# An attention phase whose chances are divided by their sum before they are split and transposed, not after

## The chip, the core and the metric

The kernel runs on one core of a Trainium2 chip. The metric is the device time of one execution in microseconds (us); the kernel before takes 1757.22 us in the median of three runs (1755.55 to 1758.23). A measurement of this kernel can tell about 0.2%, 3.5 us, from no change.

The names of the engines are those of the profile: PE is TensorE's matmul and PEld its weight load, DVE is VectorE, ACT is ScalarE, POOL is GpSimd and SP is SyncE, which here only issues DMAs ("SPq"). Each engine takes its instructions strictly in the order of the program; an instruction that waits for a semaphore holds all behind it on its engine.

## The reference

Four sequences ("batches") of 512 tokens of width 1024, with 64 context tokens each, pass through cross attention and a quantised gated network, each behind a layer norm and with a residual:

```
x = x + attention(layernorm(x), context)      # 16 heads of 96, 4 groups of keys and values
x = x + ffn(layernorm(x))                     # weights and activations rounded to 8-bit steps, inner width 2752

hidden = concatenate([context, latents])      # 64 + 512 rows
q = latents @ Wq.T ; k = hidden @ Wk.T ; v = hidden @ Wv.T
attn = softmax((q . k) / sqrt(96))            # 512 x 576 for each head
out  = (attn . v) @ Wo.T

s = max(max(|t|) / 127, 1e-8)                 # fake_quant, row by row
q = clip(round(t / s), -128, 127) * s
```

## The kernel before, in words

The program has two phases with a barrier between them: `attention_phase` (until 1248 us of the profiled execution) and `ffn_phase`. The change lies in the first.

**Precision.** Matrix operands are float16 pairs: a value is written as a high part and the rest, a low part, and a product of two such operands is three matmuls (hi.hi, hi.lo, lo.hi). So everything that TensorE reads has to be split: ScalarE writes the high half (an `activation` with a float16 output), VectorE or GpSimd subtracts it from the float32 value and writes the low half.

**Work of a batch.** `batch_order(b)` writes TensorE's order out by hand, in 18 steps. Step j holds the four score tiles of head j (`score_tile`, 128 queries against 576 keys, into two PSUM tensors `ps_s` in turn), the product of the chances of head j - 2 with the values (`pv_tile`, into the one bank `ps_o`), and side work that fills the time: projections of values, queries and keys for later heads or for the next batch and the output projection of finished groups (`V`, `Q`, `K`, `WO`), in three banks `ps_g`. The first score tile stands first in a step, the others at quarters of the step's remaining work. Steps 16 and 17 have no scores.

**A tile of chances** passes: scores in `ps_s` -> VectorE's row maximum (L1113) -> ScalarE's exp in float32 into `p_f`, of which there are NF = 2, with the row's sum (L1006) -> ScalarE's exp a second time, in float16, into `p_nat` (L1012), after which the score bank is free -> GpSimd's subtraction in two pieces (L791, L792) -> a DMA transpose of the pair, from SP, into `pT` (L686). `p_nat` has NN = 4 places, so a tile's place is that of the same tile of the head before, and L1012 waits until that one's transpose has landed. The chances aren't yet divided by their sum. That is done at the end of a head: the reciprocals of the four sums (L1120) go to DRAM (`inv_out`, L690) and come back spread over 96 partitions (`inv_in`, L697, which waits on SP for the write's landing), and VectorE multiplies the head's output by them (`normalise`, L1131); then the output is split by ScalarE (L1021) and GpSimd (`out_lo`, L797).

**Weights of the second phase** are quantised beside this, in 52 units (`("w", g)`): SP loads a unit into one of two buffers `w_in` (`stage`), VectorE finds its scale (L1143 to L1154), ScalarE divides and adds a constant that rounds (`lift`, L976), VectorE takes the constant off and writes `w_int` (`round`, L1161), SP transposes it (`turn`, L641) and writes the result to DRAM (`keep`, L652). There is one `w_int`, so L1161 waits until the transpose before has landed. The weights of the attention pass the same two buffers in batch 0 (`split`, `cache`).

**The order on each engine** is a sorted list: `engine_events()` gives each operation a planned time, worked out from a rough cost of TensorE's own work (`pe_times`), and each engine executes its operations in the order of their planned times. `stage_events()` plans the weights, `token_events()` the layer norm, split and transpose of the next batch's tokens, which fall around step 11. These times only set the order; what an operation waits for are its semaphores.

**TensorE's waits** at the places touched: a score tile waits for `p_done` of the tile two before it (L902), the first `pv_tile` of a head for its four transposes and for `ps_o` to be free (L917 to L919).

## Time and profile before

| | |
|---|---|
| median of three runs | 1757.22 us (1755.55 to 1758.23) |
| the profiled execution | 1757.65 us |
| its span, first to last instruction | 1755.9 us |
| attention phase, to the border | about 1248.7 us |
| PE busy | 1567.4 us (89% of the span) |
| DVE, ACT, POOL busy | 1036.7, 655.3, 515.5 us |
| mean granted clock of TensorE | 0.955 |

How to read it: "busy" is the time in which an engine had an instruction in work. The clock is given as a share of 2.4 GHz and has two levels, 1.00 and 0.50 (1.2 GHz); a figure between them is a mean over a stretch. A "DMA share" is the mean busy share of the core's 16 DMA engines; it can pass 1 a little, since packets overlap. A wait is told as "who waited <- for what", with the sum, the number of times and the longest. SP issues DMAs, so the time of an "SPq" row is that of the issue, not of the transfer.

### The profile page before, as it was taken

The numbers are of one execution on the slowest core, as the hardware profiler recorded it, in microseconds if no ns is written. First come the engines' busy times: TensorE is split into PE (matmuls) and PEld (weight loads), VectorE is DVE, ScalarE is ACT, GpSimd is POOL, SyncE is SP. The second block draws the span as 40 slices with busy tenths as digits, with TensorE's granted clock in tenths as the row PEclk, the third lists the DMA queues.
The fourth block names the chain that finished last, engine by engine and source line by source line (L and its number), as shares of the span: only waits on it lengthen the run. The fifth ranks groups of instructions, "written<-read, shape, count | busy, mean of one in ns | idle before, by whom it ended". The sixth has DMA issues, their size and how long they took to land. (4 is left out here: it accounts for less than half of the span.)

```text
span 1755.9 us, 23588 instructions
## 1 busy us (share of the span) xinstructions
PE 1567.4 (89%) x8084; PEld 773.3 (44%) x8084; DVE 1036.7 (59%) x1760; ACT 655.3 (37%) x1180; POOL 515.5 (29%) x635
## 2 busy tenths in 40 slices
PE   6989989999877999888799788898579999999997
PEld 3544434654333465443346334443234444444443
DVE  5346554345555434555444445465379999898984
ACT  3456553256544225555422455452211111111110
POOL 3356653045445214445521244452000000000000
PEclk9999999999898999999999899999789999999998
DMA  7499999699999969999986999998863333324232
GB/s 233 116 249 237 240 231 233 185 212 228 226 227 230 200 173 222 239 209 230 222 200 187 263 218 205 207 202 199 263 227 85 91 89 86 95 80 105 70 93 64
DMA packets 546185, 323.62 MB, mean 184 GB/s; under 512 B 484144, under 2 KB 491056, under 8 KB 544944
## 3 DMA queue, kind: packets, MB, share of 16 engines
q1 hardware_dynamic: 546096, 322.49, 77.2%
q8 instruction: 50, 0.82, 0.2%
q14 instruction: 39, 0.32, 0.1%
HBM read 151.78 MB, written 46.79 MB: 113 GB/s over the span
## 5 line engine op out<-in xcount | busy, mean ns | idle before, releaser
L791 POOL TENSOR_TENSOR p_nat<-p_f,p_nat 128x512 f16<-128x512 f32 x256 | 300.6, 1174 | 478.9 <-ACT p_nat L1012 478.4
L1113 DVE TENSOR_REDUCE small<-ps_s 128x1 f32<-128x576 f32 x256 | 192.8, 754 | 257.2 <-PE ps_s L908 255.7
L907 PE MATMUL ps_s<-k,q 96*128 96x512 f16 x768 | 231.2, 393 | 95.4 <-ACT p_nat L1012 95.4
L1006 ACT ACTIVATE p_f<-ps_s,small 128x576 f32<-128x576 f32 x256 | 189.2, 739 | 267.5 <-DVE small L1113 265.5
L1012 ACT ACTIVATE p_nat<-ps_s,small 128x576 f16<-128x576 f32 x256 | 188.5, 736 | 133.3 <-DMA pT<-p_nat 132.7
L1391 PE MATMUL ps_gu<-w_gu_sb,xT 128*128 128x512 bf16 (+1 forms) x1152 | 230.8, 361 | 0.0
L1432 ACT ACTIVATE g_sb<-g_sb,sx 128x512 f32<-128x512 f32 (+1 forms) x128 | 74.5, 582 | 390.6 <-DVE g_sb L1503 331.5
L1404 PE MATMUL ps_d<-w_dn_sb,hT 128*128 128x512 bf16 x704 | 161.5, 383 | 5.4 <-DMA hT<-h_int 5.4
L907 PEld LDWEIGHTS ps_s<-k,q 96*128 96x128 f16 x768 | 76.2, 99 | 201.7 <-issue 82.1
L1391 PEld LDWEIGHTS ps_gu<-w_gu_sb,xT 128*128 128x128 bf16 x1152 | 112.8, 98 | 115.4
L922 PE MATMUL ps_o<-pT,v_lo 128*96 128x512 f16 x320 | 133.4, 417 | 33.0 <-DMA pT<-p_nat 32.9
L908 PE MATMUL ps_s<-k,q 96*128 96x64 f16 x768 | 150.1, 196 | 0.0
L818 PE MATMUL ps_g<-wo,o 128*128 128x512 f16 x384 | 148.9, 388 | 1.1 <-POOL o L797 1.1
L819 PE MATMUL ps_g<-wo,o 128*128 128x512 f16 x384 | 148.6, 387 | 0.0
L820 PE MATMUL ps_g<-wo,o 128*128 128x512 f16 x384 | 148.5, 387 | 0.0
L818 PE MATMUL ps_g<-xnT,wq 128*128 128x512 f16 x384 | 146.3, 381 | 1.4 <-DMA xnT<-xh 0.7
L820 PE MATMUL ps_g<-xnT,wq 128*128 128x512 f16 x384 | 146.2, 381 | 0.0
L819 PE MATMUL ps_g<-xnT,wq 128*128 128x512 f16 x384 | 146.1, 380 | 0.0
L1370 POOL TENSOR_TENSOR rstd<-var_eps,minus_half 128x1 f32<-128x1 f32 x16 | 8.8, 550 | 460.1 <-DVE var_eps L1473 460.1
L1174 DVE SCALAR_TENSOR_TENSOR x_acc<-ps_g,x_acc 128x512 f32<-128x512 f32 x128 | 88.1, 689 | 86.7 <-PE ps_g L820 86.5
L797 POOL TENSOR_TENSOR o<-o_tmp,o 96x512 f16<-96x512 f32 x64 | 75.6, 1182 | 194.8 <-ACT o L1021 194.8
L923 PE MATMUL ps_o<-pT,v_hi 128*96 128x512 f16 x320 | 130.1, 407 | 0.0
(113 smaller groups left out, 2403.6 us busy)
## 6 DMA issues: line engine op xcount, KB each, us to landing
w_in<-w_gu SPq DMA_DIRECT2D x40, 512.0 KB, 4.7
wq<-wq_c SPq DMA_DIRECT2D x36, 512.0 KB, 4.9
wo<-wo_c SPq DMA_DIRECT2D x24, 768.0 KB, 5.6
inv_sum<-inv_d SPq DMA_DIRECT2D x64, 192.0 KB, 3.4
gu_q<-w_t SPq DMA_DIRECT2D x44, 256.0 KB, 4.1
w_in<-w_dn SPq DMA_DIRECT2D x8, 1376.0 KB, 7.1
w_gu_sb<-gu_q SPq DMA_DIRECT2D x3, 2816.0 KB, 12.8
x_acc<-x SPq DMA_DIRECT2D x4, 2048.0 KB, 8.9
```

The source lines that it names most:

```text
L791: nc.gpsimd.tensor_tensor(n[:, S + C:2 * S], f[:, 0:T], n[:, 0:T], ALU.subtract)
L818: nc.tensor.matmul(o, l_hi, r_hi, start=(first and i == 0), stop=False)
L819: nc.tensor.matmul(o, l_hi, r_lo, start=False, stop=False)
L820: mm = nc.tensor.matmul(o, l_lo, r_hi, start=False, stop=(last and i == len(pairs) - 1))
L907: nc.tensor.matmul(o[:, 0:T], l, k2[0:HD, hl, kv, 0:T], start=(i == 0), stop=(i == 2))
L908: mm = nc.tensor.matmul(o[:, T:S], l, k2[0:HD, hl, kv, T:S], start=(i == 0), stop=(i == 2))
L922: nc.tensor.matmul(o, v_lo[:, t, kv, :], p[:, t, :], start=(t == 0), stop=False)
L1006: nc.scalar.activation(p_f[:, t % NF, :], scores(t), ACT.Exp, bias=bias, accum_out=sums[:, j % 2, t:t + 1])
L1012: nc.scalar.activation(p_nat[:, t % NN, 0:S], scores(t), ACT.Exp, bias=bias).then_inc(p_done, 1)
L1113: nc.vector.tensor_reduce(neg_max[:, j % 2, t:t + 1], scores(t), AX.X, ALU.max, negate=True).then_inc(mx_done, 1)
L1391: mm = nc.tensor.matmul(ps_gu[n % NR][:, 0:nu * P], xT[:, k, :], w[:, u0:u0 + nu, k, :], start=(k == 0), stop=(k == KD - 1))
L1404: mm = nc.tensor.matmul(ps_d[h][:], hT[0:rows, c, :], w_dn[0:rows, 4 * h:4 * h + 4, c, :], start=(c == 0), stop=(c == IC - 1))
```

## The change

- **Chances.** The exp is done once, in float32, into one of four `p_f` (NF = 4), and frees the score bank. VectorE scales the row's sum by 2^-9 and takes its reciprocal (`invert`, now for each tile). ScalarE multiplies `p_f` by it and writes the float16 high half (`high`); GpSimd multiplies `p_f` by it in place, in float32, and then subtracts the high half. What is transposed is divided already, times 2^9.
- **Output.** `normalise`, `inv_out`, `inv_in`, `o_tmp`, the broadcast sums and the DRAM tensor are gone. ScalarE writes the high half of a head's output straight from `ps_o`, VectorE (not GpSimd) the low half.
- **Semaphores.** The splits of attention weights have their own pair (`h_up`, `h_out`) and no longer share a count with the units' `w_up` and `w_out`. `pv_tile` waits for `o_lo_s`, not for `o_mul`.
- **Order.** Planned times are later for the units' `round`, `turn` and `keep` (six microseconds, `LAND`, for each landing), for tokens (an interval of 10 in place of 8, a start 8 earlier) and for the load of output weights; the units of the last batch are planned within 0.85 of its time.

```diff
-NF = 2
+NF = 4
...
+P_UP = 2.0 ** 9
+WEIGHTS_FOR = (1.0, 1.0, 1.0, 0.85)
...
-            units.append((START[b] + (i + 0.4) * (START[b + 1] - START[b]) / UNITS[b], ("w", g)))
+            units.append((START[b] + (i + 0.4) * WEIGHTS_FOR[b] * (START[b + 1] - START[b]) / UNITS[b], ("w", g)))
...
+LAND = 6.0
+TOKEN_LEAD, TOKEN_STEP = 20.0, 10.0
...
+        for h in range(halves):
+            k = TURNS.index((g, h))
+            t = max(t, turned[-1] + LAND)
+            dve.append((t, "round", g, h))
+            wide = halves == 2 or (k and halves_of(TURNS[k - 1][0] % NUNIT) == 2)
+            t = max(t + 2.5, (kept[-1] if wide else kept[-2]) + LAND)
+            sp += [(t, "turn", k), (t + LAND, "keep", k)]
+            turned.append(t)
+            kept.append(t + LAND)
...
-                act.append((t + 1.0, "exp", b, j, k))
-                pool.append((t + 3.0, "low", b, j, k))
-                sp.append((t + 5.0, "turn_p", b, j, k))
-                if k == TT - 1:
-                    dve.append((t + 3.3, "invert", b, j))
-                    sp += [(t + 3.8, "inv_out", b, j), (t + 6.5, "inv_in", b, j)]
+                dve.append((t + 2.0, "invert", b, j, k))
+                act += [(t + 1.0, "exp", b, j, k), (t + 2.4, "high", b, j, k)]
+                pool.append((t + 3.1, "low", b, j, k))
+                sp.append((t + 6.0, "turn_p", b, j, k))
...
-                dve.append((t + 0.1, "normalise", b, j))
-                act.append((t + 1.4, "out_hi", b, j))
-                pool.append((t + 2.2, "out_lo", b, j))
+                act.append((t + 0.1, "out_hi", b, j))
+                dve.append((t + 0.9, "out_lo", b, j))
...
             def chances_lo(b, j, t):
-                f, n = p_f[:, t % NF, :], p_nat[:, t % NN, :]
-                pool.wait_ge(p_done, tile(b, j, t) + 1)
-                nc.gpsimd.tensor_tensor(n[:, S + C:2 * S], f[:, 0:T], n[:, 0:T], ALU.subtract)
-                nc.gpsimd.tensor_tensor(n[:, S:S + C], f[:, T:S], n[:, T:S], ALU.subtract).then_inc(p_low, 1)
...
+                f, h = p_f[:, t % NF, :], p_nat[:, t % NN, :]
+                pool.wait_ge(p_high, tile(b, j, t) + 1)
+                nc.gpsimd.tensor_tensor(f, f, inv_sum[:, j % 2, t:t + 1].broadcast_to([P, S]), ALU.mult).then_inc(p_scaled, 1)
+                pool.wait_ge(p_scaled, tile(b, j, t) + 1)
+                nc.gpsimd.tensor_tensor(h[:, S + C:2 * S], f[:, 0:T], h[:, 0:T], ALU.subtract)
+                nc.gpsimd.tensor_tensor(h[:, S:S + C], f[:, T:S], h[:, T:S], ALU.subtract).then_inc(p_low, 1)
...
-                nc.scalar.activation(p_f[:, t % NF, :], scores(t), ACT.Exp, bias=bias, accum_out=sums[:, j % 2, t:t + 1])
+                nc.scalar.activation(p_f[:, t % NF, :], scores(t), ACT.Exp, bias=neg_max[:, j % 2, t:t + 1],
+                                     accum_out=sums[:, j % 2, t:t + 1]).then_inc(p_done, 1)
+
+            def chances_hi(b, j, t):
+
+                act.wait_ge(inv_done, tile(b, j, t) + 1)
                 if head(b, j):
                     act.wait_ge(p_turned[t], head(b, j) * EV)
...
-                nc.scalar.activation(p_nat[:, t % NN, 0:S], scores(t), ACT.Exp, bias=bias).then_inc(p_done, 1)
+                nc.scalar.activation(p_nat[:, t % NN, 0:S], p_f[:, t % NF, :], ACT.Copy,
+                                     scale=inv_sum[:, j % 2, t:t + 1]).then_inc(p_high, 1)
...
+            def invert(b, j, t):
+                dve.wait_ge(p_done, tile(b, j, t) + 1)
+                s = sums[:, j % 2, t:t + 1]
+                nc.vector.tensor_scalar(s, s, 1.0 / P_UP, None, ALU.mult).then_inc(sum_down, 1)
+                dve.wait_ge(sum_down, tile(b, j, t) + 1)
+                nc.vector.reciprocal(inv_sum[:, j % 2, t:t + 1], s).then_inc(inv_done, 1)
+
+            def out_lo(b, j):
+                hi, lo = out_rows(j)
+                dve.wait_ge(o_hi_s, head(b, j) + 1)
+                nc.vector.scalar_tensor_tensor(lo, ps_o[0:HD, :], 1.0 / P_UP, hi, ALU.mult, ALU.subtract).then_inc(
+                    o_lo_s, 1)
```

**VectorE, last batch, between two row maxima of head 2** (`small<-ps_s` is the row maximum, `small<-w_in` and `s_w<-small` the scale of a unit, `w_int<-w_in` the rounding, `q<-ps_g` and `o_tmp<-ps_o` evacuations). Before:

```order
L1113 TENSOR_REDUCE small<-ps_s 128x1
L1103 SCALAR_TENSOR_TENSOR q<-ps_g,q 128x512
L1143 TENSOR_REDUCE small<-w_in 128x1
L1161 TENSOR_SCALAR w_int<-w_in 128x1344
L1113 TENSOR_REDUCE small<-ps_s 128x1
L1131 TENSOR_TENSOR o_tmp<-ps_o,inv_sum 96x512
L1143 TENSOR_REDUCE small<-w_in 128x1
L1149 TENSOR_TENSOR small<-small 128x1
L1152 TENSOR_SCALAR s_w<-small 128x1
L1154 RECIPROCAL small<-s_w 128x1
```

In the changed kernel, from the same maximum on (L1112 is the maximum, L1118 and L1120 the new reciprocal, L1156 the rounding, L1125 the output's low half):

```order
L1112 TENSOR_REDUCE small<-ps_s 128x1
L1102 SCALAR_TENSOR_TENSOR q<-ps_g,q 128x512
L1138 TENSOR_REDUCE small<-w_in 128x1
L1144 TENSOR_TENSOR small<-small 128x1
L1147 TENSOR_SCALAR s_w<-small 128x1
L1149 RECIPROCAL small<-s_w 128x1
L1118 TENSOR_SCALAR small<-small 128x1
L1120 RECIPROCAL small<-small 128x1
L1156 TENSOR_SCALAR w_int<-w_in 128x1344
L1112 TENSOR_REDUCE small<-ps_s 128x1
L1125 SCALAR_TENSOR_TENSOR o<-ps_o,o 96x512
L1118 TENSOR_SCALAR small<-small 128x1
```

The rounding moved behind the scale's small steps and a reciprocal that waits for the exp; it still stands in front of the same maximum.

**SP, the same stretch** (`pT<-p_nat` are the transposes of chances, `w_t<-w_int` those of weights). Before:

```order
L641 DMA_TRANSPOSE w_t<-w_int 128x11x128
L622 DMA wq<-wq_c 128x2048
L690 DMA inv_d<-small 128x4
L686 DMA_TRANSPOSE pT<-p_nat 128x9x128
L652 DMA dn_q<-w_t 128x1408
L697 DMA inv_sum<-inv_d 96x512
L641 DMA_TRANSPOSE w_t<-w_int 128x11x128
L600 DMA w_in<-w_gu 128x1024
L686 DMA_TRANSPOSE pT<-p_nat 128x9x128 x2
```

In the changed kernel:

```order
L651 DMA_TRANSPOSE w_t<-w_int 128x11x128
L689 DMA x_acc<-x 128x4x1024
L696 DMA_TRANSPOSE pT<-p_nat 128x9x128
L632 DMA wq<-wq_c 128x2048
L662 DMA dn_q<-w_t 128x1408
L696 DMA_TRANSPOSE pT<-p_nat 128x9x128 x2
L651 DMA_TRANSPOSE w_t<-w_int 128x11x128
L610 DMA w_in<-w_gu 128x1024
```

The write and the read of the reciprocals are gone from the queue; the transposes of weights stand further apart from each other.

**SP, the last rows of the attention phase** (`dn_q<-w_t` is `keep`, `x<-x_acc` the store of the result). Before:

```order
L641 DMA_TRANSPOSE w_t<-w_int 128x11x128
L652 DMA dn_q<-w_t 128x1408
L722 DMA x<-x_acc 128x4x512
L641 DMA_TRANSPOSE w_t<-w_int 128x11x128
L652 DMA dn_q<-w_t 128x1408
L722 DMA x<-x_acc 128x4x512
L641 DMA_TRANSPOSE w_t<-w_int 128x11x128
L652 DMA dn_q<-w_t 128x1408
L641 DMA_TRANSPOSE w_t<-w_int 128x11x128
L652 DMA dn_q<-w_t 128x1408
```

In the changed kernel:

```order
L662 DMA dn_q<-w_t 128x1408
L639 DMA wo<-wo_c 128x3072
L651 DMA_TRANSPOSE w_t<-w_int 128x11x128
L639 DMA wo<-wo_c 128x3072
L662 DMA dn_q<-w_t 128x1408
L651 DMA_TRANSPOSE w_t<-w_int 128x11x128
L720 DMA x<-x_acc 128x4x512
L662 DMA dn_q<-w_t 128x1408
L720 DMA x<-x_acc 128x4x512
```

Two transposes and two writes of weights stood behind the last store; none does now.

## Rows read from the trace of the kernel before

**Rows 1.** Windows, core 0: stretch, its us, each engine's busy us, clock, DMA.
```profile
65.65:283.49 217.84, 195.67 (x1044) 95.67 (x1042) 117.78 (x168) 129.20 (x239) 127.42 (x148) 0.95 1.02 228
283.49:341.58 58.09, 58.09 (x335) 33.13 (x334) 24.54 (x34) 11.05 (x16) 6.59 (x6) 1.00 0.67 199
341.58:589.14 247.56, 213.40 (x1115) 104.24 (x1114) 124.22 (x200) 128.53 (x239) 116.93 (x148) 0.93 1.01 223
647.23:896.04 248.81, 214.11 (x1116) 103.99 (x1115) 126.38 (x200) 128.21 (x239) 118.62 (x148) 0.94 1.04 226
954.13:1196.16 242.03, 205.83 (x1083) 100.46 (x1082) 120.03 (x186) 125.78 (x234) 106.48 (x138) 0.94 1.01 224
```
**Rows 2.** Waits of TensorE: waiter <- awaited: us in total, times, longest.
```profile
PE ps_s L907 <- ACT p_nat L1012: 95.4, 37, 7.2
PE ps_o L922 <- DMA pT<-p_nat: 32.9, 19, 4.4
PE ps_d L1413 <- PEq L386: 15.9, 1, 15.9
```
**Rows 3.** The same view, ScalarE and VectorE.
```profile
ACT p_nat L1012 <- DMA pT<-p_nat: 132.7, 67, 8.1
DVE small L1113 <- PE ps_s L908: 255.7, 132, 5.8
DVE w_int L1161 <- DMA w_t<-w_int: 49.6, 10, 11.0
```
**Rows 4.** Timeline around 1000 us: start us, us, instruction, [idle before].
```profile
999.71 0.86 DVE L1161 TENSOR_SCALAR w_int<-w_in 128x1344 bf16<-128x1344 f32 x1 [10.95 <-DMA w_t<-w_int]
...
1002.79 0.61 PE L907 MATMUL ps_s<-k,q 96*128 96x512 f16 x1 [7.24 <-ACT p_nat L1012]
```
**Rows 5.** Timeline, 222 to 233 us, GpSimd and SP.
```profile
222.94 0.31 POOL L792 TENSOR_TENSOR p_nat<-p_f,p_nat 128x64 f16<-128x64 f32 x1
...
232.78 1.50 SPq L686 DMA_TRANSPOSE pT<-p_nat  x1
```
**Rows 6.** Issues by line: duration ns min/median/max, first and last start.
```profile
L690 SPq DMA_DIRECT2D inv_d<-small x64: 319/572/2994, 79.0 to 1202.2; - x64
...
L697 SPq DMA_DIRECT2D inv_sum<-inv_d x64: 319/508/1708, 82.9 to 1207.8; - x64
```
**Rows 7.** Waits of the SP queue.
```profile
SPq L697 <- DMA inv_d<-small: 40.9, 24, 4.9
```
**Rows 8.** Groups by line: busy us, mean ns | idle before <-releaser.
```profile
L1006 ACT ACTIVATE p_f<-ps_s,small 128x576 f32<-128x576 f32 x256 | 189.2, 739 | 267.5 <-DVE small L1113 265.5 <-POOL p_nat L792 0.7
...
L791 POOL TENSOR_TENSOR p_nat<-p_f,p_nat 128x512 f16<-128x512 f32 x256 | 300.6, 1174 | 478.9 <-ACT p_nat L1012 478.4
...
L792 POOL TENSOR_TENSOR p_nat<-p_f,p_nat 128x64 f16<-128x64 f32 x256 | 94.0, 367 | 0.0
...
L779 POOL TENSOR_TENSOR xh<-xc,xh 128x1024 f16<-128x1024 f32 x12 | 25.5, 2125 | 0.0
...
L1131 DVE TENSOR_TENSOR o_tmp<-ps_o,inv_sum 96x512 f32<-96x512 f32 x64 | 68.3, 1067 | 38.9 <-PE ps_o L923 30.7 <-DMA inv_sum<-inv_d 8.2
```
**Rows 9.** Window of one head (batch 1, head 3) without stalls; columns of rows 1.
```profile
383.57:394.75 11.18, 11.18 (x64) 5.57 (x63) 5.20 (x8) 7.89 (x16) 6.94 (x10) 1.00 1.14 193
```
**Rows 10.** Two VectorE lines: duration ns min/median/max, first and last start.
```profile
L1161 DVE TENSOR_SCALAR w_int<-w_in x60: 660/694/1942, 99.9 to 1240.1; 128x1024 bf16<-128x1024 f32 x40, 128x1408 bf16<-128x1408 f32 x8, 128x1344 bf16<-128x1344 f32 x8, 96x1024 bf16<-96x1024 f32 x4
...
L1152 DVE TENSOR_SCALAR s_w<-small x52: 149/153/155, 91.4 to 1229.4; 128x1 f32<-128x1 f32 x48, 96x1 f32<-96x1 f32 x4
```
**Rows 11.** Timeline around the border of the phases, SP.
```profile
1233.53 0.38 SPq L722 DMA_DIRECT2D x<-x_acc  x1
...
1245.88 0.33 SPq L652 DMA_DIRECT2D dn_q<-w_t  x1
...
1248.79 0.33 SPq L1307 DMA_DIRECT2D x_ln<-x  x1
```
**Rows 12.** DMA issues: count, KB each, us from issue to landing.
```profile
x<-x_acc SPq DMA_DIRECT2D x8, 1024.0 KB, 7.4
```

More of the change, by code:

```diff
@@ L217, in item_halves, with lifts, split_no @@
     return halves_of(i[1] % NUNIT) if i[0] == "w" else 1
-def ups(i, half=0):
-    return sum(item_halves(k) for _, k in STAGE[:ITEM[i]]) + half + 1
-def freed(n):
-    return ups(STAGE[n][1], item_halves(STAGE[n][1]) - 1)
+def lifts(g, half=0):
+    return sum(halves_of(i % NUNIT) for i in range(g)) + half + 1
+def split_no(n):
+    return sum(1 for _, i in STAGE[:n + 1] if i[0] != "w")
 def smalls(g, k):
@@ new lines, in stage_events @@
+        for h in range(halves):
+            act.append((t, "lift", g, h))
+            t += 3.0
+        lifted = t
+        t -= 3.0 * (halves - 1)
+        for h in range(halves):
+            k = TURNS.index((g, h))
[6 more added lines that the diff above has]
+            kept.append(t + LAND)
@@ L540, in staged, with freed @@
             eng.wait_ge(w_in_s[n % 2], (n // 2 + 1) * EV)
+        def freed(eng, n):
+            kind, *a = STAGE[n][1]
+            if kind == "w":
+                eng.wait_ge(w_out, lifts(a[0], halves_of(a[0] % NUNIT) - 1))
+            else:
+                eng.wait_ge(h_out, split_no(n))
         def split_to(n):
@@ L847, in v_proj @@
                         pe.wait_ge(ctx_lo, 1)
-                        pe.wait_ge(w_out, freed(ITEM["wv", part]))
+                        freed(pe, ITEM["wv", part])
                 if part == 0:
@@ L1033, in context_hi @@
                 nc.scalar.activation(xnT_hi[:, :, T:S], ctx_in, ACT.Copy).then_inc(ctx_hi, 1)
-            run = {"split": w_split, "lift": lift, "evac": evac, "exp": chances, "out_hi": out_hi,
+            run = {"split": w_split, "lift": lift, "evac": evac, "exp": chances, "high": chances_hi, "out_hi": out_hi,
                    "tokens_hi": tokens_hi, "context_hi": context_hi}
```

133 lines of the change are left out of this document (48 added, 85 removed).

## The prediction

> **What bounds the kernel now.** I read the table of windows first, since one profile holds four alike batches and then a second phase. In it the reader is to see that a batch has two kinds of stretch. From a batch's first score tile to its last (218, 248, 249 and 242 us, 956 us together) TensorE is busy 196, 213, 214 and 206 us, so it stands idle 127 us; between the batches it is busy for all of 58.09 us [rows 1]. The clock column says the same a second time: 0.95, 0.93, 0.94 and 0.94 in those stretches against 1.00 between them, so (1 - clock) x length = 11 + 17 + 15 + 15 = 58 us of full speed are lost to time at 1.2 GHz, behind the idle gaps [rows 1]. The whole loss, 185 us, is what an edit of these stretches can win; the second phase isn't touched but for its start.
>
> Next, who is waited for. TensorE waits 95.4 us in 37 places for the second exp of a tile, since a score bank is free only after it, and 32.9 us in 19 places for a transposed chance tile: 128 us, all of the idle time above [rows 2]. Neither is a slow instruction. ScalarE had itself waited 132.7 us in 67 places to start that second exp, for the transpose that frees its place in `p_nat`, and VectorE waited 49.6 us in ten places, once 11.0 us, for the transpose of weights that frees `w_int` [rows 3]. The longest of these shows how it reaches TensorE: the rounding at L1161 sat 10.95 us at the head of VectorE's queue, the row maximum stood behind it, and TensorE idled 7.24 us [rows 4]. So both are transposes that come late. The third view says why: at 222.94 GpSimd ends its part of a tile (0.31 us), and the transpose of that tile is issued at 232.78, some 9.5 us later [rows 5]. **The SP queue is what is late**: it carries everything, and the DMA engines behind it are full, share 1.01 to 1.04 in the four stretches against 0.67 between them [rows 1].
>
> **The change, part by part.**
>
> *No reciprocals through DRAM.* 64 writes at a median of 0.572 us and 64 reads at 0.508 us leave the SP queue [rows 6], 69 us, and with them 40.9 us in which SP stood waiting for the write to land [rows 7]. That is 110 us in 64 heads, 1.7 us a head, against a head of about 15 us. SP is behind by several us, so this comes off the lateness of each transpose that follows.
>
> *The chances are split later, the scores freed earlier.* A score bank is now free after the first exp. That saves one pass of 0.739 us [rows 8], and, which weighs more, a late transpose now holds the copy `high` of tile n while the exp of n is done already: TensorE may run one tile further, 11.18/4 = 2.8 us in a head without stalls [rows 9]. Against it the chain from scores to transpose grows: the reciprocal in two small VectorE steps (0.15 us each by [rows 10]) and one pass of GpSimd over 128x576 in float32. No row shows that pass. From 64 to 512 columns GpSimd's subtraction goes from 367 to 1174 ns, 1.80 ns a column [rows 8], so 576 columns make 1.29 us; 1024 columns at 2.125 us [rows 8] give 1.2 us in proportion. The float32 output and the operand that is broadcast could make it cheaper (0.37 us, one small pass, is the lower bound) or dearer (2.125 us, the longest pass there is, the upper one). I take 1.29, as the nearest row is the same kind of operation. The chain is then some 1.6 us longer, about what SP gets back per head.
> Of the 95.4 us, 37 waits, mean 2.6 us, I take 60% as gone (57 us): the mean wait is as long as the tile of room, but VectorE's eleven-microsecond kind is longer. Of the 32.9 us I take half (16 us): these wait for the chain itself, which SP shortens and GpSimd lengthens. **Together -73.** The clock follows the gaps: 73/128 of 58 us, **-33**.
>
> *Rounding moved back.* The table of order puts `round` behind the time at which the last transpose should have landed. In the place shown it stands behind the whole scaling of the next weight and a reciprocal, but still in front of the same maximum; so this kind of wait is cut and not abolished, and I count it within the 60%.
>
> *GpSimd.* Per tile 1.29 + 1.17 + 0.37 = 2.83 us instead of 1.54; its part of the output (`out_lo`) goes to VectorE. 64 tiles make 181 us a stretch, four token tiles at 2.13 us 8.5 more: 190 us, where TensorE at full clock would need 213.40 x 0.93 = 198 us in the second stretch and 186 to 201 in all. That is level. In a head that has but one Q unit beside it TensorE needs 11.18 us [rows 9] and GpSimd 4 x 2.83 = 11.3 with its handovers on top, half a microsecond dearer; there are 7 such heads in a batch, 28: 14 us. 12 token tiles of 2.13 us fall in the same place, half of them on the path: 13 us. Sum 27, **+30** in round numbers. Nothing hides this once SP no longer does; it is the next bound.
>
> *VectorE.* 256 x 2 x 0.15 = 78 us are added, 64 multiplications at 1.067 us (68 us [rows 8]) give way to 64 subtractions of the same size, priced between 0.7 of them and all: +58 to +78 on 488 us busy of 956 [rows 1]. They are hidden while VectorE has room. The new wait is not so harmless: the reciprocal waits for the exp of its own tile (0.739 us and the read of the sum), and behind it in the queue stand the evacuations of `ps_g` and the sums into `x_acc`, for which TensorE waits. At most 256 x 0.739 = 189 us of standing and the reads on top, mostly beside time that was idle (255.7 us of VectorE's idle time, in 132 waits, are for scores [rows 3]). I take **+8**, between 0 and 80.
>
> *A rule weighed.* Large VectorE passes do meet GpSimd: the rounding takes 694 ns in the median and up to 1942 [rows 10]. The small scaling L1152 took 149 to 155 ns in all 52 places, though GpSimd was busy for half of these stretches [rows 1, 10]; so the 256 new small ones are priced as they stand. The Trainium skill, "SBUF — State Buffer", section "SBUF: two separate sides", says that VectorE in a two-port mode and GpSimd take their shared ports as an exclusive lock and that the loser blocks for the whole instruction. The trace of the rounding agrees; whether a one-column pass asks for the lock the page does not say, and L1152 speaks against it. It is a rival below.
>
> *End of attention.* The last batch's weights come at 0.85 of their place, so the last `round` and `keep` stand ahead of the last sums and stores instead of behind them. Now TensorE waits 15.9 us at the phase's border [rows 2]: the last store is issued at 1233.53, but SP has weights to write until 1245.88, and the load of the second phase's first tokens goes out at 1248.79 [rows 11]. Then it could go out when the store has landed, 7.4 us after its issue [rows 12]: 1240.9, **-8**. What would be late next is that store.
>
> *Other counters of the weights, loads, query and output orders:* the same instructions, 0. Had they wrong places, a wait on the staging of a weight would appear; the SP queue's slack covers it.
>
> **Sum**, against the profiled execution of 1757.65 us (span 1755.9, 1.75 around it; the median of three is 0.43 lower): -73 - 33 + 30 + 8 - 8 = -76, so 1681.7, and in terms of the median **1681 us**.
>
> **Rivals.**
> 1. *The DMA engines set the pace.* For: share 1.01 to 1.04. Against: two stretches alike in share differ in length, and SP stands waiting 40.9 us for one small write. The reads and writes removed are 64 x 194 KB = 12.4 MB, of some 225 GB/s x 956 us = 215 MB: 5.8%, at most 55 us. I price it at 40, with the end -8: 1709. Chance 0.22.
> 2. *VectorE stands behind the exp.* ScalarE held at `high` holds the next exp, that holds the reciprocal, that holds an evacuation, and TensorE waits for a bank. With 80 us instead of 8: 1753. Chance 0.08, spread over all three signs.
> 3. *Slower: GpSimd's new pass.* The stretches have 956/256 = 3.73 us a tile, so from 3.73 - 1.54 = 2.19 us for the pass on GpSimd alone is slower than all of it was. At 2.4 us: 256 x 3.94 + 26 for tokens = 1035 us instead of 956, with the end +71: 1828. Against: it would be 1.9 times the estimate. Chance 0.06.
> 4. *The small passes take the lock.* 256 times half a GpSimd pass (0.6 us) at half the chance of meeting one = 77 us of VectorE, half on the path: 1719. Chance 0.04. (That is the Trainium skill's rule of the section named above.)
> 5. *Better than forecast.* The lateness of SP vanishes as a whole, the stretches stand near GpSimd's and TensorE's floors, 200 + 3 x 215 = 845 us: -111 - 8, 1638. Chance 0.14.
>
> **How the numbers follow.** The forecast has 0.46, between 1650 and 1712. The range of 1640 to 1745 leaves out most of the better case's lower half, rival 3 and most of rival 2, under 2 in 10. A measurement here tells 0.2% (3.5 us) from no change. Faster: 0.46 + 0.22 + 0.14 + 0.04 + 0.02 = 0.88; same 0.03; slower 0.06 + 0.03 = 0.09.
>
> **What would show it.** Stretches of 218, 248, 249 and 242 us should become about 205, 228, 228 and 222, the clock in them 0.97. ScalarE's wait for `pT` should halve, and the wait of TensorE name the first exp. A GpSimd pass over 128x576 at 1.3 us, GpSimd busy 190 us a stretch. SP should show fewer rows and a transpose 2 to 5 us after its tile. TensorE's wait at the border should be some 2 us. I'm wrong if TensorE's waits name `ps_g` (rival 2), if the pass takes 2 us (rival 3), or if the transposes are as late as before with an SP queue that is 110 us lighter (rival 1).

## The result, and the profile after

The changed kernel takes 1688.36 us in the median of four runs (1685.0 to 1690.25), beside 1756.38 us of the kernel before on the same chip: ratio 0.961, 95% interval 0.9592 to 0.9629. The profiled execution took 1685.0 us, its span is 1683.2 us, its mean granted clock 0.964. The two profiled executions lie 72.7 us apart, the medians 68.0; where a profile is split up below, its own difference is meant.

**Where the 72.7 us of span went.** The four stretches from a batch's first score tile to its last, with one stretch between batches as the last row (columns as in [rows 1]):

```profile
65.74:282.78 217.04, 196.52 (x1045) 96.44 (x1043) 129.54 (x277) 132.90 (x238) 182.59 (x195) 0.94 0.98 217
340.87:571.23 230.36, 208.46 (x1116) 102.83 (x1115) 140.66 (x309) 131.54 (x238) 175.66 (x195) 0.96 0.98 224
629.32:858.46 229.14, 208.94 (x1115) 102.68 (x1114) 139.47 (x309) 132.35 (x238) 175.53 (x195) 0.96 1.01 232
916.55:1137.37 220.82, 203.60 (x1083) 100.36 (x1082) 138.42 (x308) 131.58 (x235) 164.23 (x185) 0.95 1.04 246
282.78:340.87 58.09, 58.09 (x335) 33.20 (x334) 24.70 (x37) 11.68 (x17) 6.61 (x6) 1.00 0.62 187
```

The stretches sum to 897.4 us, where those of [rows 1] sum to 956.2: -58.9. TensorE's busy time in them fell from 829.0 to 817.5 us, though its instructions are the same (I put that down to the clock, -11.5: its four figures went from 0.95, 0.93, 0.94 and 0.94 to 0.94, 0.96, 0.96 and 0.95), and its idle time from 127.2 to 79.8 (-47.4). Between batches nothing moved, 58.09 us both times. After the last score tile attention ends 2.1 us sooner, the way from the last matmul into `ps_g` to the first into `ps_gu` fell from 30.2 to 19.0 us (-11.2), and the second phase moved by 0.7. Batch 0 hardly gained: 217.84 to 217.04.

**Who waits for whom.** The waits that answer [rows 2] and [rows 3]; line numbers are those of the changed kernel (L999 the exp, L1010 `high`, L1112 the row maximum, L1118 and L1120 the reciprocal, L1156 the rounding):

```profile
PE ps_s L903 <- ACT p_f L999: 39.2, 21, 5.9
PE ps_o L918 <- DMA pT<-p_nat: 39.5, 17, 5.5
PE ps_d L1408 <- PEq L388: 2.0, 1, 2.0
...
ACT p_nat L1010 <- DMA pT<-p_nat: 35.6, 15, 6.1
ACT p_nat L1010 <- DVE small L1120: 113.7, 162, 4.1
DVE small L1118 <- ACT p_f L999: 121.6, 140, 4.3
DVE small L1112 <- PE ps_s L904: 110.6, 92, 4.7
DVE w_int L1156 <- DMA w_t<-w_int: 21.2, 8, 5.2
```

TensorE's wait for a score bank fell from 95.4 to 39.2 us, but its wait for a transposed tile rose from 32.9 to 39.5. ScalarE's wait for a place in `p_nat` fell from 132.7 to 35.6 us, and in its place stand two waits that are new: VectorE at the head of its queue for the exp (121.6 us), ScalarE for the reciprocal (113.7 us). The groups that answer [rows 8]:

```profile
L790 POOL TENSOR_TENSOR p_f<-p_f,small 128x576 f32<-128x576 f32 x256 | 299.2, 1169 | 373.3 <-ACT p_nat L1010 372.5
...
L792 POOL TENSOR_TENSOR p_nat<-p_f,p_nat 128x512 f16<-128x512 f32 x256 | 312.5, 1221 | 20.1
L1010 ACT ACTIVATE p_nat<-p_f,small 128x576 f16<-128x576 f32 x256 | 195.5, 774 | 149.7 <-DVE small L1120 113.7 <-DMA pT<-p_nat 35.6
L1118 DVE TENSOR_SCALAR small<-small 128x1 f32<-128x1 f32 x256 | 38.3, 149 | 122.6 <-ACT p_f L999 121.6
```

And what answers [rows 5], GpSimd's end of a tile and the issue of its transpose:

```profile
282.30 0.31 POOL L793 TENSOR_TENSOR p_nat<-p_f,p_nat 128x64 f16<-128x64 f32 x1
...
282.68 1.75 SPq L696 DMA_TRANSPOSE pT<-p_nat  x1
```

The transpose now follows its tile by 0.07 us (282.61 to 282.68) where one shown before came 9.5 us later. Over all 256 tiles, from the starts and ends of the rows of these two lines, the mean fell from 5.13 to 1.52 us. GpSimd's own part of a tile took 2.78 us instead of 1.50, and from the end of a tile's scores to the landing of its transpose it is 14.4 us instead of 16.1.

At the border, what answers [rows 11]: the last store, the first load of the second phase (4.2 us after the store's issue in place of 15.3), and TensorE:

```profile
1172.67 0.39 SPq L720 DMA_DIRECT2D x<-x_acc  x1
1176.90 0.34 SPq L1302 DMA_DIRECT2D x_ln<-x  x1
...
1173.87 1.06 PE L1408 MATMUL ps_d<-ident,s_w 128*128 128x128 f32 x8 [1.96 <-PEq L388]
```

### The profile page after: what moved, and what is told of

Same layout as the page of the kernel before. It is cut to its first block and busy times, and to the rows that moved or that the text cites. A ratio compares the mean times of both kernels' runs of the same rounds, so it can differ in the third digit from the quotient of the medians.

```text
span 1683.2 us, 24162 instructions
## 1 busy us (share of the span) xinstructions
PE 1552.1 (92%) x8084; PEld 770.0 (46%) x8084; DVE 1086.0 (65%) x2208; ACT 670.2 (40%) x1180; POOL 745.3 (44%) x827
## 5 line engine op out<-in xcount | busy, mean ns | idle before, releaser
L790 POOL TENSOR_TENSOR p_f<-p_f,small 128x576 f32<-128x576 f32 x256 | 299.2, 1169 | 373.3 <-ACT p_nat L1010 372.5
L792 POOL TENSOR_TENSOR p_nat<-p_f,p_nat 128x512 f16<-128x512 f32 x256 | 312.5, 1221 | 20.1
L999 ACT ACTIVATE p_f<-ps_s,small 128x576 f32<-128x576 f32 x256 | 188.4, 736 | 209.0 <-DVE small L1112 208.3
L1112 DVE TENSOR_REDUCE small<-ps_s 128x1 f32<-128x576 f32 x256 | 192.3, 751 | 111.9 <-PE ps_s L904 110.6
L903 PE MATMUL ps_s<-k,q 96*128 96x512 f16 x768 | 226.0, 387 | 39.4 <-ACT p_f L999 39.2
L1010 ACT ACTIVATE p_nat<-p_f,small 128x576 f16<-128x576 f32 x256 | 195.5, 774 | 149.7 <-DVE small L1120 113.7
L918 PE MATMUL ps_o<-pT,v_lo 128*96 128x512 f16 x320 | 132.6, 414 | 39.6 <-DMA pT<-p_nat 39.5
L814 PE MATMUL ps_g<-wo,o 128*128 128x512 f16 x384 | 147.1, 383 | 0.0
L816 PE MATMUL ps_g<-wo,o 128*128 128x512 f16 x384 | 147.0, 383 | 0.0
L815 PE MATMUL ps_g<-wo,o 128*128 128x512 f16 x384 | 147.0, 383 | 0.0
```

Source lines behind the costliest of these rows:

```text
L790: nc.gpsimd.tensor_tensor(f, f, inv_sum[:, j % 2, t:t + 1].broadcast_to([P, S]), ALU.mult).then_inc(p_scaled, 1)
L792: nc.gpsimd.tensor_tensor(h[:, S + C:2 * S], f[:, 0:T], h[:, 0:T], ALU.subtract)
L814: nc.tensor.matmul(o, l_hi, r_hi, start=(first and i == 0), stop=False)
L815: nc.tensor.matmul(o, l_hi, r_lo, start=False, stop=False)
L816: mm = nc.tensor.matmul(o, l_lo, r_hi, start=False, stop=(last and i == len(pairs) - 1))
L903: nc.tensor.matmul(o[:, 0:T], l, k2[0:HD, hl, kv, 0:T], start=(i == 0), stop=(i == 2))
```

## The experiments

The theories. **A**: SyncE's queue with the reciprocals' round trip made the transposes late, and taking it out is the gain. **B**: the early release of the score bank is. **C**: the planned times (orders) are. **D**, rival 1 of the prediction: what counts of the round trip is the work of the DMA engines. The runs fall into five groups on different chips, and each group has its own runs of the kernel before (medians of 1753.3 to 1756.6 us). So all are put on one footing, ratio x 1756.4 us, with the interval of the ratio, and every +, - and difference below is on that footing:

| kernel | ratio | 95% interval | us on one footing |
|---|---|---|---|
| before | 1 | | 1756.4 |
| changed | 0.961 | 0.9592 to 0.9629 | 1687.9 |
| orders_only | 0.9789 | 0.9773 to 0.9806 | 1719.3 |
| old_orders | 0.9818 | 0.9802 to 0.9834 | 1724.4 |
| before_no_trip | 0.9603 | 0.9583 to 0.9623 | 1686.7 |
| trip_back | 0.995 | 0.9933 to 0.9966 | 1747.6 |
| orders_no_trip | 0.942 | 0.9374 to 0.9467 | 1654.5 |
| trip_small | 0.9788 | 0.9744 to 0.9831 | 1719.2 |
| late_release | 0.9696 | 0.9654 to 0.9738 | 1703.0 |
| no_mult | 0.9474 | 0.9427 to 0.952 | 1664.0 |
| old_tokens | 0.9663 | 0.962 to 0.9706 | 1697.2 |
| sums_from_pe | 0.9812 | 0.9768 to 0.9856 | 1723.4 |
| vector_mult | 0.9555 | 0.9513 to 0.9598 | 1678.2 |
| vector_later | 0.9513 | 0.9496 to 0.953 | 1670.9 |

### The planned times, alone and taken back

`orders_only` is the kernel before with these lines (and the new `stage_events` and `token_events`, and the separate counters for the attention weights that they need):

```diff
-            sp.append((filled_at(*out_done(n - 2)) + 0.3, "out_w", n))
+            sp.append((filled_at(*out_done(n - 2)) + 1.5, "out_w", n))
...
+WEIGHTS_FOR = (1.0, 1.0, 1.0, 0.85)
```

> The kernel before with the planned times of the changed one for weights, tokens, output weights and the last batch (and the separate counters that these times need), but its own path of the chances: two exps, two p_f, the division after the product, the reciprocals through DRAM. Theory A (SyncE's queue: the removed round trip makes the transposes earlier) gives this part only the end of the attention phase: -10 us, 1746, with the stretches still at 956 us. Theory B (early release of the score bank) says the same, 1746. Theory C (the orders bring the gain, since rounding no longer stands in front of a row maximum for a landing) says -40 or more, 1716 or less, and TensorE's waits behind the exp down from 95 to under 60 us.

Measured: 1716.07 us, 37 us less than before, close to what theory C says. Its profile, 44.2 us shorter than that of the kernel before, has stretches of 924.1 us together (-32.1) and a border shorter by 11.2. TensorE's wait behind ScalarE is still 78.7 us, not under 60. What did change is SyncE's own waits. Of the kernel before (L629 the load of output weights, L652 `keep`, L639 `turn`):

```profile
SPq L629 <- PE ps_g L820: 43.4, 11, 7.4
...
SPq L652 <- DMA w_t<-w_int: 33.7, 18, 3.8
SPq L639 <- DMA dn_q<-w_t: 20.9, 10, 5.5
```

and of `orders_only`, where these lines are L654, L677 and L664:

```profile
SPq L654 <- PE ps_g L845: 14.5, 5, 5.9
...
SPq L677 <- DMA w_t<-w_int: 10.9, 6, 3.5
SPq L664 <- DMA dn_q<-w_t: 5.3, 1, 5.3
```

67 us in which SyncE stood at the head of its queue with transposes of chances behind it are gone (98.0 to 30.7). The wait that I had meant, VectorE's for the place in `w_int`, did not fall: 49.6 us in ten places became 59.2 in 19, though the longest is 7.7 in place of 11.0. That SyncE's three waits are what the 37 us came from is my reading; no run changes them alone, and the mean time from GpSimd's end of a tile to the issue of its transpose fell only from 5.13 to 4.23 us.

`old_orders` takes the orders out of the changed kernel:

```diff
-WEIGHTS_FOR = (1.0, 1.0, 1.0, 0.85)
+WEIGHTS_FOR = (1.0, 1.0, 1.0, 1.0)
...
-            sp.append((filled_at(*out_done(n - 2)) + 1.5, "out_w", n))
+            sp.append((filled_at(*out_done(n - 2)) + 0.3, "out_w", n))
```

> The changed kernel with the planned times of the one before for weights, tokens, output weights and the last batch; its path of the chances is kept. Theories A and B: +10 us for the end of the attention phase and a little for the rounding that again stands in front of a maximum, 1698 to 1705. Theory C: +40 or more, 1728 or above. If this and the opposite edit don't add up to the whole difference of 68 us, the parts need each other.

Measured: 1722.1 us, +36, and TensorE waits 16.3 us at the border again. SyncE's three waits are back too, 106.3 us together (L626 the load of output weights, L649 `keep`, L636 `turn`):

```profile
SPq L626 <- PE ps_g L803: 49.8, 11, 12.2
...
SPq L649 <- DMA w_t<-w_int: 36.1, 20, 5.0
...
SPq L636 <- DMA dn_q<-w_t: 20.4, 10, 5.3
```

So the orders are worth 36 to 37 us in either kernel; theory C holds for over half of a gain that it shares. Where the time lies differs: of the 37.1 us between the profiles of this pair, 22.7 lie behind the last score tile (11.3 of them at the border) and 14.5 in the stretches. `old_tokens` puts back only `token_events` and the place of `out_w`:

> The changed kernel with the old planned times for the tokens (interval 8, start 8 later) and the load of output weights only; those of the weights of the second phase and of the last batch are the new ones. It splits the 34 us that all orders together are worth in the changed kernel. If the rounding and its transposes carry them: under +6, 1694 or less. If the tokens do: +15 or more, 1703 or above.

Measured: 1697.06 us, +9, and its interval just touches that of the changed kernel. That lies between the two cases set beforehand. SyncE's wait for the output weights' buffer is 39.8 us again, beside 17.8 in the changed kernel. Most of the 36 us belongs to the orders of the weights and of the last batch, but the tokens' share is known only as some +1 to +17 us by the two intervals.

### The round trip through DRAM

`before_no_trip`:

```diff
-                    sp += [(t + 3.8, "inv_out", b, j), (t + 6.5, "inv_in", b, j)]
...
-                    dve.wait_ge(inv_out_s, (head(b, j) - 1) * EV)
...
-                dve.wait_ge(inv_in_s[j % 2], (head(b, j) // 2 + 1) * EV)
...
+            nc.vector.memset(inv_sum[:], 1.0)
```

> The kernel before without the write and the read of the reciprocals; the head's output is multiplied by a constant tensor of ones, so that the division by the sum is left out and the output isn't the reference's. Everything else is as before: two exps, late release of the bank, old orders, GpSimd with one subtraction. Theory A: most of what the change won in the stretches, -45 us, 1711, and the time from GpSimd's end to the issue of a transpose falls from 5.1 to under 3 us. Theory B: at most -15, 1741 or more. Theory C: at most -15 as well.

Measured: 1683.93 us, -70. By itself this is worth as much as the whole change, far more than the 45 us expected. The stretches are 206.9, 228.3, 231.1 and 215.4 us. From GpSimd's end of a tile to the issue of its transpose the mean fell from 5.13 to 2.85 us, as expected, and TensorE's two waits from 128 to 72 us:

```profile
PE ps_s L906 <- ACT p_nat L1011: 55.4, 27, 5.9
PE ps_o L921 <- DMA pT<-p_nat: 16.4, 8, 2.8
```

This kernel doesn't divide, and its VectorE no longer waits for the reciprocals that were read either; that wait was 8.2 us in all [rows 8]. SyncE's three waits of the section above are as long as before (45.1, 41.1 and 22.3 us). `trip_back`, the opposite:

```diff
+                    sp += [(t + 4.2, "inv_out", b, j), (t + 6.9, "inv_in", b, j)]
...
+                sp.dma_start(inv_d[j], inv_sum[:, j % 2, :]).then_inc(inv_out_s, EV)
...
+                sp.wait_ge(inv_out_s, (head(b, j) + 1) * EV)
...
+                sp.dma_start(inv_wide[0:HD, 0, :], inv_d[j].rearrange("p t -> (p t)").partition_broadcast(HD))
```

> The changed kernel with the write and the read of the reciprocals put back on SyncE's queue at the end of each head, with the wait for the write's landing; nobody uses what is read, the output is the changed kernel's. The queue carries 110 us more again, in rows and waits of the kernel before. Theory A: +40 us or more, 1728. Theory B: +12 or less, 1700, since the bank is released ahead of the transposes whatever SyncE does. Theory C: +12 or less as well. A third of the way (+15 to +30) would say that A and B share the gain.

Measured: 1744.82 us, +60. No engine waits for what is read (VectorE only lets the write finish before it overwrites the reciprocals two heads on), so the price lies with the queue and the transfers. `trip_small` tells these two apart as far as it can (beside `trip_back`, the ends of the lines left out here and above):

```diff
-                sp.dma_start(inv_wide[0:HD, 0, :], inv_d[j].rearrange("p t -> (p t)").partition_broadcast(HD))
+                sp.dma_start(inv_wide[0:1, 0, :], inv_d[j].rearrange("p t -> (p t)").partition_broadcast(1))
```

> The changed kernel with the round trip put back as in trip_back (1745 us), but the read goes to one partition (2 KB) instead of 96 (192 KB a head, 12.4 MB in all). SyncE has the same write, wait and issue; the DMA engines have next to nothing to move for it. If the cost of the trip is SyncE's time and its wait (theory A), 1735 to 1745. If it is what the DMA engines move (rival 1 of the prediction), 1690 to 1705. Half-way, 1710 to 1725, both.

Measured: 1717.59 us, half-way. Of `trip_back` and of `trip_small`, the packets of the queue, SyncE's wait for the write, and TensorE's two waits:

```profile
q1 hardware_dynamic: 546096, 322.49, 77.1%
...
SPq L711 <- DMA inv_d<-small: 41.0, 19, 4.6
...
PE ps_o L935 <- DMA pT<-p_nat: 61.3, 31, 6.7
PE ps_s L920 <- ACT p_f L1016: 55.5, 23, 5.7
```

```profile
q1 hardware_dynamic: 539056, 310.03, 75.3%
...
SPq L711 <- DMA inv_d<-small: 41.2, 22, 4.7
...
PE ps_s L920 <- ACT p_f L1016: 51.0, 23, 4.9
PE ps_o L935 <- DMA pT<-p_nat: 49.1, 26, 6.5
```

SyncE's wait is the same, and the issue of the read is only shorter by 0.14 us in the median (0.527 to 0.385 us, 9 us in all), but 12.5 MB are gone and with them 28 of the 60 us (28, give or take 8, by the two intervals). The transposes of chances show both parts: in the mean they are issued 1.52 us after GpSimd's end in the changed kernel, 3.08 in `trip_back` and 2.56 in `trip_small`, and they land 4.44, 4.74 and 4.48 us after their issue. So theory A and rival 1 each hold for about half: 31 us for the write with its wait and a small read, 28 us for the broadcast, 12.5 MB that the DMA engines moved at a share near 1. Bytes, packets (7040 fewer) and the 9 us of issue went together in this run, so what each is worth isn't shown.

### Both parts without the new path of the chances

`orders_no_trip` has the edits of `orders_only` and of `before_no_trip` together; like the latter it leaves out the division.

> The kernel before with both other parts of the change: the new planned times (37 us alone) and no write and read of the reciprocals (69 us alone; the output is multiplied by ones, so the division is left out and the output isn't the reference's). Its path of the chances stays: two exps, late release, one subtraction on GpSimd. If the two parts are independent, 1753 - 37 - 69 = 1647 and the new path of the chances then costs the changed kernel some 40 us; theory A now says this, with 1650 to 1665, since both parts cut the same lateness. If the early release of the bank pays for GpSimd's pass (theory B), this kernel is no faster than the changed one, 1685 or above.

Measured: 1654.07 us. -37 and -70 would make -107, both together make -102: they are nearly independent. And it is 33 us faster than the changed kernel: **the new path of the chances costs 33 us**, give or take 9, and is the price for dividing without the round trip. The next runs take this price apart. `late_release`:

```diff
                 if tile(b, j, t) >= 2:
-                    pe.wait_ge(p_done, tile(b, j, t) - 1)
+                    pe.wait_ge(p_high, tile(b, j, t) - 1)
```

> The changed kernel, but a score tile waits for the high half (p_high) of the tile two before it instead of the exp: the bank is held as long as in the kernel before, across the reciprocal and ScalarE's copy, though nothing reads it. Theory B (early release): +15 us or more, 1703 or above, and TensorE's waits behind ScalarE grow by 20 us. Theory A: under +8, 1696 or less, since the transposes are no longer late.

Measured: 1700.97 us, +15. TensorE's waits:

```profile
PE ps_s L903 <- ACT p_nat L1010: 76.5, 51, 5.8
PE ps_o L918 <- DMA pT<-p_nat: 9.8, 9, 2.8
```

Beside the changed kernel the wait for a bank is 37 us longer and the wait for a transposed tile 30 us shorter. Early release lets TensorE run ahead with scores, and then it meets the same late chances at `ps_o`. In the stretches its idle time is 7 us longer and its busy time 5 us, 12 us in the profile, where the medians are 15 apart. `no_mult`:

```diff
-                nc.gpsimd.tensor_tensor(f, f, inv_sum[:, j % 2, t:t + 1].broadcast_to([P, S]), ALU.mult).then_inc(p_scaled, 1)
-                pool.wait_ge(p_scaled, tile(b, j, t) + 1)
```

> The changed kernel without GpSimd's multiplication, so that the low half of a chance is the undivided exp less the divided high half, and wrong; all else is there, the reciprocals and ScalarE's copy too. It prices GpSimd's pass alone. If the pass is nearly all that the new path costs (prediction: +30; the runs so far leave 34 + 12 = 46 us for it and VectorE's part): 1650 to 1658. If half of it is the reciprocal of each tile, which stands on VectorE behind the exp: 1668 to 1675, with VectorE's wait for the exp and ScalarE's for the reciprocal still over 100 us each.

Measured: 1664.69 us, -24, between the two cases set beforehand: GpSimd's pass costs 24 us. (The low halves are wrong in this kernel.) VectorE's and ScalarE's waits around the reciprocal hardly changed:

```profile
DVE small L1116 <- ACT p_f L997: 121.2, 141, 5.7
ACT p_nat L1008 <- DVE small L1118: 109.6, 165, 3.2
```

The sum: 33 = 24 (GpSimd) - 15 (early release) + a rest of 24. The rest comes from four measurements, good to 3 to 8 us each, and so is 24 give or take 14. It holds all that the other runs leave: the small VectorE steps of each tile and the waits around them, ScalarE's copy in place of a second exp, and the new end of a head. No run takes these apart. Nor is the bank of `late_release` held just as long as that of the kernel before: it stays held across the reciprocal too.

Batch 0 is now plainer: its stretch is 217.8 us before, 217.7 in `orders_only`, 206.9 in `before_no_trip`, 207.7 in `no_mult` and 217.0 in the changed kernel. The round trip's going gave 11 us there, and GpSimd's pass took 9 of them back.

### Other ways to divide

`vector_mult` gives the multiplication to VectorE (GpSimd's pass and the scale of ScalarE's copy go):

```diff
-                nc.vector.tensor_scalar(s, s, 1.0 / P_UP, None, ALU.mult).then_inc(sum_down, 1)
+                nc.vector.reciprocal(i, s).then_inc(sum_down, 1)
                 dve.wait_ge(sum_down, tile(b, j, t) + 1)
-                nc.vector.reciprocal(inv_sum[:, j % 2, t:t + 1], s).then_inc(inv_done, 1)
+                nc.vector.tensor_scalar(f, f, i, P_UP, ALU.mult, ALU.mult).then_inc(inv_done, 1)
```

> The changed kernel, but VectorE and not GpSimd multiplies p_f in place: after the reciprocal one VectorE pass over 128x576 (about 0.4 us from the 694 ns of 128x1024) times the reciprocal and 2^9, and ScalarE's high half is a plain copy of it; GpSimd keeps its two subtractions. Output as the reference. If GpSimd's pass is what the new path costs: GpSimd's busy time falls by 299 us, the chain by 0.8 us a tile, and the time by 20 to 30 us, to about 1662. If VectorE then stands in the way (100 us more on it, and large passes that meet GpSimd's took up to 1.9 us), 1690 or slower.

Measured: 1677.08 us, -10, between the two cases set beforehand; the intervals overlap by a hair, so that it is faster than the changed kernel isn't shown by this run. VectorE's pass took 520 ns in the median where I had expected 0.4 us. GpSimd is idle just over half the time in the stretches now; the longest new wait is ScalarE's for VectorE's pass.

```profile
L1118 DVE TENSOR_SCALAR p_f<-p_f,small 128x576 f32<-128x576 f32 x256 | 145.6, 569 | 9.0
...
ACT p_nat L1008 <- DVE p_f L1118: 182.8, 189, 3.1
DVE small L1116 <- ACT p_f L997: 112.0, 136, 4.7
```

`vector_later` keeps that kernel and moves planned times alone:

```diff
-                dve.append((t + 2.0, "invert", b, j, k))
-                act += [(t + 1.0, "exp", b, j, k), (t + 2.4, "high", b, j, k)]
-                pool.append((t + 3.1, "low", b, j, k))
+                dve.append((t + 2.8, "invert", b, j, k))
+                act += [(t + 1.0, "exp", b, j, k), (t + 3.4, "high", b, j, k)]
+                pool.append((t + 4.0, "low", b, j, k))
```

> The kernel of vector_mult (1677 us, VectorE multiplies), output as the reference, with later planned places for what follows the exp: the reciprocal 0.8 us, ScalarE's copy 1.0 us and GpSimd's part 0.9 us later, so that on each engine other work stands in front of them more often. If what is left of the new path's price is engines that stand at the head of their queue for the step before (VectorE for the exp, 112 us in 136 places there; ScalarE for VectorE, 183 us in 189): these two waits fall by a third or more, and the time to 1665 to 1673. If it is the longer way of a tile from scores to transpose: 1680 or slower, with more waits of TensorE for ps_o. Within 4 us of 1677 neither.

Measured: 1672.55 us in the median of five, ratio 0.9513 (0.9496 to 0.953): **faster than both kernels**, 17 us below the changed one. But the reason is half a miss: both waits were to fall by a third. VectorE's wait for the exp fell by a quarter, ScalarE's for VectorE not at all, and TensorE's own two waits are as long as in `vector_mult` (38.8 and 36.5 us beside 42.4 and 34.1). The 7 us between the two have overlapping intervals; the better order is not shown, the faster kernel is.

```profile
DVE small L1116 <- ACT p_f L997: 82.3, 108, 4.4
ACT p_nat L1008 <- DVE p_f L1118: 190.3, 157, 5.8
```

`sums_from_pe` was to get the 33 us back as a whole (`w` is all 128 rows of `ps_o`, and `v_hi` has 96 columns of values and 32 of ones for each group):

```diff
+                    nc.tensor.matmul(w, v_hi[:, t, kv, :], p[:, t, :], start=(t == 0), stop=False)
...
+                nc.vector.reciprocal(o_tmp[0:32, :], ps_o[HD:P, :]).then_inc(inv_done, 1)
...
+                nc.scalar.activation(o_tmp[32:64, :], o_tmp[0:32, :], ACT.Copy)
+                nc.scalar.activation(o_tmp[64:96, :], o_tmp[0:32, :], ACT.Copy).then_inc(inv_wide, 1)
...
+                nc.vector.tensor_tensor(o_tmp[0:HD, :], ps_o[0:HD, :], o_tmp[0:HD, :], ALU.mult).then_inc(o_mul, 1)
```

> A third way to divide, output as the reference: the chances stay undivided (one exp, a plain copy as the high half, one subtraction on GpSimd, early release of the bank, three p_f), and v_hi has 32 more columns of ones, so that the product that is there anyway also leaves the sums of a head in 32 rows of ps_o. Once a head VectorE takes their reciprocal (32x512), ScalarE copies it to two more groups of partitions, and VectorE multiplies as in the kernel before. No DRAM trip, no reciprocal for each tile, no multiplication on GpSimd; new planned times. If the new path of the chances is what costs and early release is worth 12 us: 1654 - 12 + some 5 for the longer end of a head = 1640 to 1655, the fastest of all. If the end of a head (four steps on three engines while ps_o is held) stands in TensorE's way, its waits for ps_o grow by 20 us or more and it is 1665 or slower.

Measured: 1724.85 us, a miss by 70, and not through the mechanism that I had named (TensorE waits only 16.2 us for `ps_o`). One row tells it:

```profile
L1137 DVE RECIPROCAL o_tmp<-ps_o 32x512 f32<-32x512 f32 x64 | 214.9, 3359 | 23.6 <-PE ps_o L937 22.0
...
L1130 DVE TENSOR_REDUCE small<-ps_s 128x1 f32<-128x576 f32 x256 | 190.8, 749 | 115.2 <-PE ps_s L917 114.3
L1141 DVE TENSOR_TENSOR o_tmp<-ps_o,o_tmp 96x512 f32<-96x512 f32 x64 | 43.9, 687 | 66.1 <-ACT o_tmp L1029 65.9
...
PE ps_s L916 <- ACT p_f L1014: 88.3, 51, 6.1
```

A reciprocal over 512 columns takes 3.36 us. I had taken it for a pass like the others. Row maxima stand behind it in VectorE's queue, and TensorE's wait for a score bank is 88.3 us. The idea is as good as the way to form a wide reciprocal; with that it wasn't tried.

## Why the prediction was right, and where its steps were not

The time was forecast at 1681 and is 1688.4, the range held it, and the direction was right. The sum came out in part by luck, and for other reasons than it gave. Between the two profiles TensorE's idle time in the stretches fell by 47.4 us (forecast 35: 73 less 30 and 8), its busy time by 11.5 (forecast 33, for the clock), and what stands behind the last score tile by 13.9 (forecast 8). The stretches became 217.0, 230.4, 229.1 and 220.8 us; the forecast's 205 for the first was the furthest off.

- **What bounds the kernel** held: late transposes behind a late SyncE queue. `before_no_trip` takes little else away and gains 70 us, and `trip_back` loses 60 though no engine waits for what is read.
- **"Together -73" for round trip and early release, less 30 and 8 for the new path.** Net that is -35 of TensorE's waits; its idle time fell by 47. The size of the parts was wrong. The round trip alone is worth 60 to 70 us and early release some 15, where my 57 us for the bank had leaned on the tile of room that early release gives.
- **"Of the 32.9 us I take half (16 us)"** failed in sign: the wait for chances at `ps_o` rose to 39.5 us. `late_release` shows why (9.8 us there, 76.5 at the bank): a TensorE that may run ahead waits at the next gate. For the waits for the bank 60% was right, 56 us against 57, but by `late_release` some 30 us of such waits only move to `ps_o`.
- **Planned times.** "Loads, query and output orders" stood at 0, the later rounding within the 60% without a price of its own, the end at -8. This failed most, with its reason, "the SP queue's slack covers it": all the planned times together are worth 36 to 37 us. Beside the kernel before some 12 us of that lie behind the last score tile, in the changed kernel 22.7, and the rest in the stretches. I had looked for waits of VectorE on the rounding, and in `orders_only` those did not fall; SyncE's own waits (43.4, 33.7 and 20.9 us) were in the trace, and I read only the one of the round trip, [rows 7].
- **The clock, "-33"**, should have followed from the sum's own net: 35/128 of 58 us are 16. Measured are 11.5 us of busy time. I had put the share on the 73 before the costs were taken off.
- **GpSimd, "+30"**: 24 by `no_mult`. The pass takes 1.15 us in the median (1.29 forecast, and the row to go by was that of 1024 columns, 2.125 us: 1.2). But "that is level" is wrong: GpSimd is busy 175.7 of 230.4 us in the second stretch. So I read its price as that of a link in each tile's chain, not of a bound, except in batch 0, where GpSimd is busy 182.6 of 217.0 us and the pass took 9 of the 24; no run tells the two apart elsewhere.
- **VectorE, "+8"**: at most the rest of some 24 us, give or take 14, that the runs leave for it and others. The new standing is there, 121.6 us in 140 places, and so is the one I had not counted at all, ScalarE's 113.7 us for the reciprocal. In the stretches TensorE waits only once for VectorE where `ps_g` is concerned, 2.9 us for split weights and not for a bank, so rival 2, as I had priced it, is out.
- **End of attention, "-8"**: -11.2 at the border, -2.1 before it. What is late next is the store, as said: it is issued at 1172.67 and the load behind it at 1176.90, 4.2 us later and not 7.4. That figure was the median of eight stores; this one landed 4.8 us after its issue in the kernel before too.
- **A rule weighed.** The one-column steps took 149 and 164 ns in the mean with GpSimd busy three quarters of the time. The 188 scalings (L1118) with a GpSimd instruction beside them took 151 ns, the 68 without one 147, so rival 4 is out: they weren't held. The 128x576 pass of `vector_mult` was: 520 ns for the 164 without GpSimd beside them (522 at most), 655 in the mean for the 92 with it, 2467 at most.
- **Rival 1** deserved more than its 0.22, not as an alternative but as a part: `trip_small` gives the broadcast 28 us, give or take 8, beside the 40 that I had priced for it.

The forecast's -16 for `ps_o`, its small price for the planned times and its doubled clock lie on different sides, and so the sum was only 7 us off: that closeness is luck. That SyncE's queue was what made the transposes late is borne out. With 1654 for the cheap parts and +33 for the new path, the change would have been worth half as much again without the way in which it divides.

## What to carry to other kernels

When one queue issues everything, list every wait of that queue itself and not only the transfers on it: each wait at its head delays all behind it, and the new planned times, which took 67 us of such waits away, were worth as much here as half the large edit. A small round trip through DRAM costs three times, in issue, in the wait for landing, and, where the DMA engines are near full, in the bytes of its broadcast. Work moved from the end of a head to each of its tiles adds a link to each tile's chain, and here that cost 33 us net on engines that were not full; price the links and the handovers, and not only the busy shares of engines.

## What the hardware showed that I had not expected

- VectorE's reciprocal over 512 columns took 3359 ns, 6.6 ns a column, where a multiplication over the same columns took 687; over one column it is 164 ns and looks like any other step. The Trainium skill, "VectorE: DVE Perf Modes", section "First, the fixed hardware budget", says that the reciprocal is an iterated division with a repeat count of 8; 3359/687 = 4.9 in whole instructions, and it is by far the dearest pass over 512 columns in these traces, so the trace agrees in kind.
- The same multiplication of 96x512 took 1067 ns in the kernel before [rows 8], where its second operand is read with a stride of four float32 elements (`normalise` in its code), and 687 ns in `sums_from_pe` with plain operands. The Trainium skill, "SBUF — State Buffer", section "Door 1: The DMA port swizzle (why `[64,N]` ≈ `[32,N]`)", speaks of lines of 16 bytes, of a penalty for each access that goes to a new one, and of four float32 as how far one can stride for free. That stride is 16 bytes, and 1067 beside 687 does not look free, but no run here changes the stride alone.
- GpSimd's multiplication in float32 with one broadcast column took 1147 ns in the median for 576 columns, 1.99 ns a column, less for a column than its subtraction into float16 (1156 ns in the median for 512, 2.26 ns a column).
- 12.5 MB more or less, 4% of what the queue moves, cost 28 us at a DMA share of 1.0 in the stretches. At 225 GB/s, what the stretches moved, they would take some 56 us (an estimate), so about half of their time was on the path.
